# Attention scores and their maxima on two halves of the array, output bias in the product, three steps moved between engines

## What is computed

```python
mod = (silu(c) @ wmod).reshape(4, 6, 1, 256)          # sa, ca, ga, sb, cb, gb; ga and gb kept away from 0
h = layernorm(x) * (1 + ca) + sa
q, k, v = split(h @ qkv_w + qkv_b)                     # 16 heads of 16 channels, rotary on q and k
attn = softmax(where(causal, -inf, q @ k.T * 0.25))
x = x + ga * (attn @ v @ out_w + out_b)
h = layernorm(x) * (1 + cb) + sb
x = x + gb * (experts(h) + shared_expert(h))           # 4 of 16 experts for each token, chosen by a router
```

## Time and profile before

| | |
|---|---|
| median of 3 runs | 3320.68 us (3320.06 to 3322.53) |
| the profiled execution | 3327.59 us, its span 3325.8 us |
| PE busy | 3052.6 us (92%), 17108 instructions |
| DVE busy | 2285.5 us (69%) |
| ACT busy | 1602.8 us (48%) |
| POOL busy | 1314.5 us (40%) |
| granted TensorE clock, mean of the span | 0.972 of full speed |
| chain that ended last | PE 68%, DVE 17%, POOL 5% |

### The profile page before, as it was taken

How to read it: one execution, slowest core, us unless ns; L and a number is a source line. 1 busy time by engine, 2 the same in 40 slices (tenths; PEclk the granted TensorE clock), 3 DMA queues, 4 the chain that set the end, 5 groups by cost and what they waited for, 6 DMA issues and landing times.

```text
span 3325.8 us, 50278 instructions
## 1 busy us (share of the span) xinstructions
PE 3052.6 (92%) x17108; PEld 1493.8 (45%) x17108; DVE 2285.5 (69%) x4981; ACT 1602.8 (48%) x2593; POOL 1314.5 (40%) x1684
## 2 busy tenths in 40 slices
PE   7777599999999999999999999998899989999998
PEld 4433133334433334333333433334666666666666
DVE  7888388887788887799997778832473224444487
ACT  3322456665566665466555466674233333333333
POOL 6756111224522124421125647634205654333275
PEclk9989799999999999899999999999999999999999
DMA  5832623222311321321323335324226655554486
GB/s 167 203 111 86 122 36 54 50 55 55 90 38 33 56 63 50 81 43 27 56 54 104 105 84 142 95 95 135 86 89 209 205 184 149 145 149 142 130 237 199
DMA packets 279623, 350.21 MB, mean 105 GB/s; under 512 B 58488, under 2 KB 236296, under 8 KB 279112
## 3 DMA queue, kind: packets, MB, share of 16 engines
q1 hardware_dynamic: 248492, 271.79, 31.5%
q0 software_dynamic: 30208, 71.87, 7.4%
q10 hardware_dynamic: 672, 3.34, 0.4%
HBM read 206.51 MB, written 139.21 MB: 104 GB/s over the span
## 4 chain that ended last, share of the span: by engine, by line
PE 68%; DVE 17%; POOL 5%; issue 4%; DMA 4%; ACT 2%; SPq 1%; ACTq 0%; DVEq 0%; POOLq 0%
PE PB L934 13%; PE PB L975 13%; PE PB L1037 12%; PE PB L956 10%; DVE mx L1338 10%; PE PB L1064 8%; PE PB L987 3%; POOL yg L1688 3%; PE PB L1050 2%; PE PB L1026 2%; PE PB L905 1%; PE PB L937 1%; DMA KO<-qk_parts 1%; DMA yg<-y_slots,sidu 1%; DVE xn L1291 1%
## 5 line engine op out<-in xcount | busy, mean ns | idle before, releaser
L1338 DVE TENSOR_REDUCE mx<-PB 128x1 f32<-128x512 f32 (+3 forms) x2560 | 1406.3, 602 | 252.2 <-PE PB L937 149.8
L1508 ACT ACTIVATE P<-PB 128x1024 f32<-128x1024 f32 (+3 forms) x1280 | 1100.7, 895 | 771.8 <-PE PB L956 768.7
L934 PE MATMUL PB<-KO,QO 96*128 96x512 bf16 (+3 forms) x2560 | 896.6, 355 | 86.4 <-DVE mx L1338 52.8
L956 PE MATMUL PB<-QO,KO 98*128 98x512 bf16 (+3 forms) x2560 | 819.9, 352 | 15.1 <-DVE PB L1363 11.6
L975 PE MATMUL PB<-P,V 128*17 128x512 f32 (+3 forms) x5120 | 601.2, 542 | 17.3 <-POOL P L1625 16.8
L934 PEld LDWEIGHTS PB<-KO,QO 96*128 96x128 bf16 x2560 | 250.1, 98 | 756.3 <-DVE mx L1338 505.3
L1037 PE MATMUL PB<-W,xT 128*128 (+1 forms) x1400 | 522.8, 497 | 21.1 <-issue 20.6
L1625 POOL TENSOR_SCALAR_AFFINE_SELECT P<-P 128x256 f32<-128x256 f32 x512 | 207.3, 414 | 563.1 <-ACT P L1508 558.5
L1430 DVE TENSOR_TENSOR ha<-sl,PB 128x192 f32<-128x192 f32 x350 | 123.7, 354 | 437.4 <-ACT sl L1553 436.3
L1688 POOL DMA_INDIRECT yg<-y_slots,sidu x256 | 245.4, 959 | 333.4 <-DVE acc L1422 175.4
L1064 PE MATMUL PB<-W,haT 96*128 (+1 forms) x1400 | 366.1, 384 | 10.5 <-DVE yo L1440 5.2
(11 more groups left out here) (162 smaller groups left out, 2836.8 us busy)
## 6 DMA issues: line engine op xcount, KB each, us to landing
xq<-x_slots SPq DMA_DIRECT2D x286, 128.0 KB, 2.5
qk_parts<-pt SPq DMA_DIRECT2D x192, 128.0 KB, 2.4
KO<-qk_parts SPq DMA_DIRECT2D x96, 256.0 KB, 5.1
y_slots<-yo SPq DMA_DIRECT2D x191, 128.0 KB
rden<-rden_rows SPq DMA_DIRECT2D x256, 64.0 KB, 2.0
QO<-qk_parts SPq DMA_DIRECT2D x16, 768.0 KB, 7.8
...
```

The source lines that it names most:

```text
L934: mm = pe.matmul(PB[:, bank, 0:n], QO[0:96, k3, j, 128 * t:128 * t + 128], KO[0:96, k3, j, 512 * kc:512 * kc + n], start=True, stop=True)
L956: mm = pe.matmul(PB[:, j, 0:n], KO[0:98, k3, j, 128 * kt:128 * kt + 128], QO[0:98, k3, j, q0:q0 + n], start=True, stop=True)
L1338: dve.tensor_reduce(mx[:, j, t, kc:kc + 1], PB[:, u.bank[item], 0:n], AX.X, ALU.max).then_inc(s["mx"], 1)
L1508: act.activation(P[:, pbuf(g, i, p), :, 0:n], PB[:, 2 * p:2 * p + 2, 0:n], ACT.Exp, scale=0.25).then_inc(s["exp"], 1)
```

## The change

**Row layout.** Products of 64 rows or fewer now stand on one half of the array: rows 0 to 63 or rows 64 to 127. For even heads, rows 0 to 63 of `QO` and `KO` hold the four products of high and middle parts, and rows 64 to 97 hold high x low, low x high and the two rows of maxima; for odd heads the halves are swapped. `loadg` is 20 DMAs in place of 9 for the same bytes (2 heads each).

**Maxima.** A `max` product has 64 rows, those of high and middle parts alone. Heads 2p and 2p+1 alternate tile by tile, so the items alternate between the halves. The mask is two products of 64 rows (L983 of 128 columns, L984 of 64 columns). `neg` and `nturn` work on two heads at once.

**Scores.** `st` becomes `sa` (64 rows, L1003) and `sb` (34 rows, L1016, adds to the same bank from the other half, so it waits for the semaphore `sa`). `sa` and `sb` of heads 0 and 1 belong to the next step (`ahead`), those of heads 3 and 2 to this one. The maxima of group g+1 now start at step 37 of group g-1.

**Other engines.** The output bias is row 16 of the projection's weights (`wo_s`) against the row of `ON` that holds the sum of probabilities over itself, so the VectorE addition becomes an ACT copy (`xo`). The copy of the logits moves to ACT too, the first step of `o_h2` to GpSimd.

```diff
+LOADS = [(z, 64 * odd + row, odd, k, n) for odd in (0, 1)
+         for z, row, k, n in ((0, 0, 0, 2), (0, 32, 0, 2), (1, 0, 0, 1), (1, 16, 0, 1), (1, 32, 1, 1), (1, 48, 1, 1))]
+LOADS += [(z, 64 - 64 * odd + row, odd, k, 1) for odd in (0, 1) for z, row, k in ((0, 0, 2), (0, 16, 0), (1, 0, 0), (1, 16, 2))]
 def max_items(g):
-    for j in range(4):
+    for p in (0, 1):
         for t in range(16):
             for kc in range(t // 4 + 1):
-                yield ("max", g, j, t, kc)
-        yield ("neg", g, j)
-        yield ("nturn", g, j)
+                for j in (2 * p, 2 * p + 1):
+                    yield ("max", g, j, t, kc)
...
+        want = min(len(mu), max(160 * max(0, n - 10) // 26, 0) if n < 37 else 160 + 4 * (n - 36))
+        quota = (want - done) // 2 * 2
+        at = done
+        ahead = order[n + 1] if n + 1 < len(order) else None
+        if len(pend) == 2:
+            values(*pend.pop(0))
+        maxima(at + (quota + 2) // 4)
+        o("sa", g, i, 3)
+        o("sa", g, i, 2)
+        maxima(at + quota // 2)
+        if ahead:
+            o("sa", *ahead, 0)
+            o("sa", *ahead, 1)
+        o("sb", g, i, 3)
+        o("sb", g, i, 2)
+        o("exp", g, i, 1)
+        maxima(at + quota // 2 + (quota + 2) // 4)
+        if ahead:
+            o("sb", *ahead, 0)
+            o("sb", *ahead, 1)
+        maxima(at + quota)
+        if ahead:
+            o("exp", *ahead, 0)
...
                     sync.dma_start(gbB[:, :], gbias.partition_broadcast(128)).then_inc(s["l_rt"], 16)
+                    sync.dma_start(wo_s[16:17, 0, :], obB[16:17, :]).then_inc(s["l_rt"], 16)
...
-                    mm = pe.matmul(PB[:, bank, 0:n], QO[0:96, k3, j, 128 * t:128 * t + 128], KO[0:96, k3, j, 512 * kc:512 * kc + n],
+                    half = slice(64 * (j % 2), 64 * (j % 2) + 64)
+                    mm = pe.matmul(PB[:, bank, 0:n], QO[half, k3, j, 128 * t:128 * t + 128], KO[half, k3, j, 512 * kc:512 * kc + n],
                                    start=True, stop=True)
                     if kc == t // 4:
-                        mm = pe.matmul(PB[:, bank, n - 128:n], identb[:, :], m1[:, :], start=False, stop=True, skip_group_check=True)
+                        pe.matmul(PB[:, bank, n - 128:n], pick[half, 0, :], tri[half, 0, :], start=False, stop=True, skip_group_check=True)
+                        mm = pe.matmul(PB[:, bank, n - 64:n], pick[half, 1, :], tri[half, 1, 64:128], start=False, stop=True,
+                                       skip_group_check=True)
...
-                    mm = pe.matmul(PB[:, j, 0:n], KO[0:98, k3, j, 128 * kt:128 * kt + 128], QO[0:98, k3, j, q0:q0 + n],
-                                   start=True, stop=True)
-                    if j % 2:
-                        mm.then_inc(s["st"], 1)
+                    rows = slice(64 * (j % 2), 64 * (j % 2) + 64)
+                    q.wait_ge(s[f"l_g{k3}"], 16 * NL * (g // 3 + 1))
+                    if o.n("exp", g, i, p) > 2:
+                        q.wait_ge(s["exp"], o.n("exp", g, i, p) - 2)
+                    pe.matmul(PB[:, j, 0:n], KO[rows, k3, j, 128 * kt:128 * kt + 128], QO[rows, k3, j, q0:q0 + n],
+                              start=True, stop=False).then_inc(s["sa"], 1)
+                elif name == "sb":
...
+                    rows = slice(64 - 64 * (j % 2), 98 - 64 * (j % 2))
+                    q.wait_ge(s["sa"], o.n("sa", g, i, j))
+                    q.wait_ge(s[f"w_nm{p}"], 64 * (g + 1))
...
+                    pe.matmul(PB[:, j, 0:n], KO[rows, k3, j, 128 * kt:128 * kt + 128], QO[rows, k3, j, q0:q0 + n],
+                              start=False, stop=True).then_inc(s["st"], 1)
...
-                    dve.tensor_tensor(xo[:, i % 2], PB[:, u.bank[item], 0:256], obB[:, :], ALU.add).then_inc(s["xo"], 1)
...
-                    dve.tensor_scalar(h2t[:, i % 3], xin[:, i % XI], mvf[:, k, 0:1], rsf[:, k:k + 1], ALU.subtract,
-                                      ALU.mult).then_inc(s["xn2"], 1)
...
-                    dve.tensor_copy(L[:, i, :], PB[:, u.bank[item], 0:16]).then_inc(s["L"], 1)
...
+                    act.activation(xo[:, i % 2], PB[:, u.bank[item], 0:256], ACT.Copy).then_inc(s["xo"], 1)
...
+                    act.activation(L[:, i, :], PB[:, u.bank[item], 0:16], ACT.Copy).then_inc(s["L"], 1)
...
+                    pool.tensor_scalar(h2t[:, i % 3], xin[:, i % XI], mvf[:, k, 0:1], rsf[:, k:k + 1], ALU.subtract,
+                                       ALU.mult).then_inc(s["xn2"], 1)
```

More of the change, by code:

```diff
@@ L139, in plan, with maximum @@
     total = None
+    def maximum(item):
+        unit(*item)
+        g, j, t, kc = item[1:]
+        if (j % 2, t, kc) == (1, 15, 3):
+            o("neg", g, j // 2)
+            turns.append([3, ("nturn", g, j // 2)])
+        else:
+            for x in list(turns):
+                x[0] -= 1
+                if x[0] == 0:
+                    turns.remove(x)
+                    unit(*x[1])
+    turns = []
     def between(c, k):
@@ L182, in plan @@
         if c == 5:
-            for part in range(9):
+            for part in range(NL):
                 o("loadg", 0, part)
@@ L191, in plan @@
     while early:
-        unit(*early.pop(0))
+        maximum(early.pop(0))
+    while turns:
+        unit(*turns.pop(0)[1])
     o("attend")
@@ L861, in expert @@
                     half = i // RB % 2 * RB
-                    pe.load(pe_regs[half:half + k], tile_e[p][0:1, i:i + k])
+                    pe.load(pe_regs[half:half + k], tile_e[p][:, i:i + k])
                     for j in range(k):
```

242 lines of the change are left out of this document (125 added, 117 removed).

## The result

The changed kernel takes 3288.43 us (3285.36 to 3291.18, four runs) against 3320.86 of the kernel before in the same job. The ratio is 0.9899, with an interval of 0.9886 to 0.9911. So it is 1.0% faster where 2.1% was forecast (3252 us). The profiled execution has a span of 3289.4 us against 3325.8.

A forecast was written before the change was run, and what follows sets the result against it. PE was taken to bound most attention groups, VectorE the two of the router. Terms -44 - 30 - 8 + 12 - 2 + 3 = -69 gave 3258.6 us profiled, 3252 us as median (6.9 lower); range 3160 to 3345.

The forecast's parts named there:

- PE's work after, full overlap of halves: Attention step on PE: products on the two row halves run together, so PE needs 2.14 us, 0.37 less than 2.51.
- ACT's loop: Full attention step: two exponentials (1.94 us) plus 0.69 dead time make 2.63 us, longer than PE's 2.36 and VectorE's 2.24.
- rival 3: Attention: ACT's dead time is hidden or shorter, VectorE's 2.24 us a step decides, kernel at 3152 us; chance 0.14.
- Groups 3, 4, 7, 8, 11, 12: 6 x -5: Attention groups with projection tiles: PE bounds tile steps, copies and bank waits give back some 0.3 us a tile; -30 us.
- GpSimd's `o_h2`: 0 in the sum: One operation more a tile on GpSimd, taken at 0.73 us, covered by idle time: 0, at the very most 47 us.
- Groups 13 and 14 as plain groups: Attention groups 13 and 14 counted with groups 1, 2, 5, 6: -7.4 us each.
- Group 15: +12: Attention group without maxima: ACT's loop no longer hidden, from 93.7 to 105 us, +12.
- Groups 9 and 10: Router groups of the attention: VectorE's 111.5 us busy is the floor of 120.1, half the idle saved; -8 us together.
- group 0: First attention group: -4 us in its other 29 steps, +2 for loads that land later, net -2.
- stage 1: Ahead of the attention: more load issues, doubled masks and changes between halves and full rows, 0 to +6 us, taken +3.
- Copies on ACT: Copies of `xo` and logits stand between exponentials; with bank waits some 0.3 us a projection tile, 5 us in group 15.
- the bias row: Output bias as a row of `wo_s`: one DMA of 1 KB ahead of group 0, cost 0.

The follow-up runs named there:

- same_half: whole_scores_h2_vector with a head's maxima ordered tile row by tile row, mostly neighbours on one half of the array: 3357.09 us, ratio 1.0092.
- swap: Changed kernel with only the next step's two `sa` of heads 0 and 1 moved behind the exponential of heads 2 and 3: 3302.53 us, ratio 0.9934.
- whole_scores: Changed kernel with each score product in one piece over all rows, no `sa` and `sb`, maxima on halves two at a time: 3257.25 us, ratio 0.9805.
- whole_scores_h2_vector: whole_scores with the first step of `o_h2` back on VectorE: 3246.27 us, ratio 0.9761.
- light_scatter: Changed kernel with scatter's indirect DMAs at 0.7 a step in groups 13 and 14 instead of 1.7: 3292.44 us, ratio 0.9906.
- h2_vector: Changed kernel with the first step of `o_h2` back on VectorE: 3272.34 us, ratio 0.9850.

## Why the prediction was right in direction and wrong in size

- *PE's work after, full overlap of halves.* Right: starts in pairs, and 111 us more without it (`same_half`).
- *ACT's loop.* Right in its mechanism and nearly in its price: 2.67 in place of 2.63. 24 x 0.04 is 1 us of a plain group's 1.6 that are missing; the rest is in narrow steps. Counted as the forecast counts (from one exponential of heads 2 and 3 to the next), 512 followed by 384 takes 2.30 (2.36 forecast), and the other twelve 2.11 to 2.57, where VectorE was to hold them at 2.24. What the step did not say is that other limits stand close behind it: `swap` takes the loop away and gains nothing, and `whole_scores` takes both kinds of wait away and gains 0.6 us a plain group, with PE's maxima then waiting for VectorE. So rival 3's 3152 us was never to be had by a shorter loop alone. The page that rival 3 named, "TensorEngine Tiling (Array Packing)" of the Trainium skill, PSUM Bottleneck, agrees with `whole_scores_h2_vector` in kind (85.8 us of waits for VectorE), though a group takes 100.4 us and not 92.
- *Groups 3, 4, 7, 8, 11, 12: 6 x -5.* **This failed, by 19 us.** Groups 3, 7 and 11 gave -15.9 as forecast, the other three +5.3. The step treated a tile as the same wherever it stands and looked at PE and VectorE only. Of the 20 us that groups 4, 8 and 12 miss, 15 stand in two steps of each, at the end of the projection, where PE waits for GpSimd and the clock falls (18.4 us in place of 13.9 in group 4). At two items a step these groups give back 7.7, 8.5 and 8.3.
- *GpSimd's `o_h2`: 0 in the sum.* **Failed.** The operation takes 1.23 us and not up to 0.73, and the cover that was named (36% busy in group 3) was the mean of another, thinner group. It costs 15 to 16 us, within the 47 given for a lost cover. This is part of the 19 above and not a further term.
- *Groups 13 and 14 as plain groups.* **Failed, by 11 us.** They were nearly plain before (109.5 and 110.4), with 7.6 us of PE's waits for GpSimd's cuts; now these are 14.4. With fewer scatters there the waits fall to 0.6 and the groups to 101.4 and 100.0 (`light_scatter`).
- *Group 15: +12.* The sign was right, 9 short. Six steps with a tile take 3.94 and not 3.66 (1.7 us); one step takes 6.47, and 3.57 in `h2_vector` (2.9 us, GpSimd again). The first 14.6 us hold five steps, and 10.2 of them are at 1.2 GHz (0.65), behind PE's gaps of 1.2 and 0.6; in the kernel before, they had 1.00 and nearly eight steps:

```profile
2139.60:2154.20 14.60, 12.18 (x88) 2.75 (x87) 0.25 (x1) 7.70 (x12) 4.99 (x12) 0.65 0.02 3
```

- *The granted clock: not in the sum.* The span's mean went from 0.972 to 0.967 of full speed. By the two levels that is about 186 us at 1.2 GHz before and 217 now, 13.7 of the difference in group 15. If PE bounds all of it, it is worth up to 16 of the 33 us missing, an estimate from these numbers. It stands inside the terms above and not beside them.
- *Groups 9 and 10, group 0, stage 1.* The first came 3 better and the second 2 worse, for causes that are open (the forecast's own 3.5 against 3.3 us in 29 steps is -6 and not -4). Stage 1 came 7 better and the experts 4.6. Both vary as much among kernels that don't differ there: the attention starts at 339.6 to 344.1 us in those with `sa` and `sb`, and what follows it takes 1032.5 to 1040.2. *Copies on ACT* and *the bias row*: no cost, as forecast.

The three failed terms miss by 19 + 11 + 9 = 39 us, the plain groups by 6 more, and the rest brings back 12 (69 - 36 = 33). GpSimd is behind most of the first two and some 3 us of the third. With the tiles spread the kernel measures 3255, by the forecast's own sum 3252; that is partly luck, since groups 13 to 15 keep their loss and groups 9 to 11 gain.
